# First down product moved behind the next tile's second up product in the early expert steps

## The reference, cut to what matters

```python
x = _layernorm(x, g, b)
x1 = x @ W1 + b1
x2 = jnp.clip(x @ W2 + b2, -20.0, 20.0)
hidden = jnp.clip(x1 * (x2 * jax.nn.sigmoid(x2)), -10000.0, 10000.0)
return jnp.clip(hidden @ Wo + bo, -10000.0, 10000.0)
```

## Time and profile before

| | |
|---|---|
| median of three timed runs | 592.98 us (592.62 to 595.98) |
| profiled execution, its own time | 591.37 us |
| span of the profiled execution | 589.6 us |
| busy share PE / DVE / ACT / POOL | 89% / 84% / 71% / 63% |
| chain that ended last: PE, DVE, issue, ACT | 58%, 16%, 14%, 6% |
| expert stage, step 1 to the last down product | about 322 to 551 us |
| mean granted clock of TensorE | 0.981 |

### The profile page before, as it was taken

How to read it: one execution, slowest core, us unless ns; L and a number is a source line. 1 busy time by engine, 2 the same in 40 slices (tenths; PEclk the granted TensorE clock), 3 DMA queues, 4 the chain that set the end, 5 groups by cost and what they waited for, 6 DMA issues and landing times.

```text
span 589.6 us, 17958 instructions
## 1 busy us (share of the span) xinstructions
PE 527.6 (89%) x5148; PEld 438.5 (74%) x5148; DVE 496.1 (84%) x1548; ACT 419.5 (71%) x1179; POOL 370.9 (63%) x708
## 2 busy tenths in 40 slices
PE   3799999999999999999978888978999999999395
PEld 2577787777877778777657777867898888888295
DVE  2689999999999999999996878889888888877353
ACT  2599998898988989889777654463566666765134
POOL 4325678888888888888877646653544344333344
PEclk9899999999999999999999999998999999999789
DMA  6313213232331311311005445653666666664283
GB/s 178 56 47 81 44 40 92 53 94 50 88 87 58 92 53 48 87 58 56 30 17 173 150 121 161 187 177 107 192 202 187 182 202 203 207 192 153 90 281 94
DMA packets 78933, 68.83 MB, mean 117 GB/s; under 512 B 17092, under 2 KB 60804, under 8 KB 78836
## 3 DMA queue, kind: packets, MB, share of 16 engines
q1 hardware_dynamic: 73748, 57.77, 34.7%
q0 software_dynamic: 4320, 9.15, 4.6%
q10 hardware_dynamic: 768, 0.75, 0.4%
HBM read 52.85 MB, written 14.80 MB: 115 GB/s over the span
## 4 chain that ended last, share of the span: by engine, by line
PE 58%; DVE 16%; issue 14%; ACT 6%; DMA 3%; ACTq 1%; another core or an unknown queue 0%; SPq 0%; DVEq 0%; POOL 0%; POOLq 0%
PE ps_m L845 7%; PE ps_t L785 5%; PE ps_s L785 5%; PE ps_s L825 4%; PE ps_s L827 4%; PE ps_t L827 3%; PE ps_t L825 3%; DVE hid L1461 3%; DVE rinv L1201 3%; PE ps_m L730 2%; ACT sil L1090 2%; PE ps_m L700 2%; PE ps_m L720 2%; PE ps_m L682 2%; PE ps_m L761 2%
## 5 line engine op out<-in xcount | busy, mean ns | idle before, releaser
L845 PEld LDWEIGHTS ps_m<-wot,hid 128*128 128x128 f32 x568 | 83.9, 192 | 20.4 <-issue 7.7
L578 POOL DMA_INDIRECT expert_out<-yt,dest x71 | 70.7, 996 | 43.8 <-issue 23.8
L845 PE MATMUL ps_m<-wot,hid 128*128 128x128 f32 x568 | 91.2, 280 | 7.0 <-DVE yt L1472 3.4
L1025 ACT ACTIVATE sc<-sc,rowmax 128x128 f32<-128x128 f32 x256 | 77.9, 389 | 1.0 <-DVE rowmax L1195 1.0
L1195 DVE TENSOR_REDUCE rowmax<-sc 128x8 f32<-128x1024 f32 x64 | 76.8, 1203 | 0.3 <-issue 0.3
L549 POOL DMA_INDIRECT expert_in<-xhat,pos x64 | 65.0, 1015 | 16.1 <-issue 15.4
L1083 ACT ACTIVATE x2c<-ps_s,prt 128x256 f32<-128x256 f32 (+1 forms) x78 | 35.4, 454 | 54.3 <-PE ps_s L827 48.3
L502 POOL TENSOR_TENSOR sc<-sc,rowmax 128x1024 f32<-128x1024 f32 x32 | 60.7, 1895 | 10.0 <-DVE rowmax L1195 8.7
L1083 ACT ACTIVATE x2c<-ps_t,prt 128x256 f32<-128x256 f32 (+1 forms) x78 | 35.3, 452 | 34.1 <-PE ps_t L827 28.1
L825 PE MATMUL ps_s<-xg,w2t 128*128 128x256 f32 (+1 forms) x156 | 46.5, 380 | 8.5 <-DVE hid L1461 6.7
L568 POOL COPY bot<-bo_rows 128x128 f32 x39 | 11.7, 301 | 60.8 <-DVE yt L1472 60.7
(11 more groups left out here) (283 smaller groups left out, 1576.7 us busy)
## 6 DMA issues: line engine op xcount, KB each, us to landing
w2t<-in_L_ffn_W_dram SPq DMA_DIRECT2D x39, 256.0 KB
w1t<-in_L_ffn_W_dram SPq DMA_DIRECT2D x39, 256.0 KB
wot<-in_L_ffn_Wo_dram SPq DMA_DIRECT2D x39, 256.0 KB
kbd<-key_image SPq DMA_DIRECT2D x29, 256.0 KB
xst<-expert_in SPq DMA_DIRECT2D x32, 137.0 KB
g<-expert_out SPq DMA_DIRECT2D x7, 512.0 KB, 9.1
call<-in_ctx_dram SPq DMA_DIRECT2D x8, 256.0 KB
out_dram<-xall SPq DMA_DIRECT2D x16, 128.0 KB, 1.8
```

The source lines that it names most:

```text
L578: pool.indirect_dma_start(ys_dram[:, :], bass.IndirectOffsetOnAxis(ap=dest[:, n, a:a + 1], axis=0), yt[:, par, a, :], None).then_inc(y_out ...
L845: mm = pe.matmul(ps_y(i)[:, a * P:(a + 1) * P], hid[:, par, c, a * P:(a + 1) * P], wot[:, par, c, :], start=(c == 0 and a == 0), stop=(c = ...
L1025: done = act.activation(sc[:, slot, h, :], sc[:, slot, h, :], ACT.Exp, bias=rowmax[:, slot, h:h + 1])
```

## The change

In steps 1 to 7 TensorE's first down product, of the tile before, is not made behind the first up products but behind the second ones, straight ahead of the second down product. From step 8 on nothing is changed, and no other engine's program differs.

```diff
--- before.py
+++ after.py
@@ -887,7 +887,10 @@
                     for c in range(CH):
                         if has(i, 0):
                             p_up(i, c, par)
-                        if has(i, 1):
+
+                        if has(i, 1) and not (c == 0 and i < MIXED):
+                            if c == 1 and i < MIXED:
+                                p_down(i - 1, 0, 1 - par)
                             p_down(i - 1, c, 1 - par)
                         if c == 1 and has(i, -1):
                             rows(i + 1)
```

## The result

The changed kernel takes 589.66 us (median of 11 runs, 587.45 to 592.52) where the kernel before, run between them on the same chip, takes 592.92 (11 runs, 591.35 to 595.98): ratio 0.9941, 95% interval 0.992 to 0.9963, or 3.5 us less (2.2 to 4.7). Two later comparisons of the same pair gave 0.995 (0.9919 to 0.998) and 0.9945 (0.992 to 0.997). The gain is real and it is half a per cent.

What follows compares the result with a forecast made beforehand. TensorE was taken to bound the kernel, with waits for VectorE's yt in the expert stage. Steps 2 to 7 summed 0.15 + 1.4 + 0.3 + 0.75 + 0 + 0.65 = 3.25 us, taking 592.98 to 589.7 us; range 586.5 to 594.0.

Steps and rivals of the forecast that it cites:

- step 3: Expert stage, step 3: Exp's table load does not wait for gmax, so Exp starts 1.56 us earlier; adds 1.4 us.
- step 4: Expert stage, step 4: gap 0.73 us, but L718 newly waits some 0.35 us for gA; adds 0.3 us.
- step 6: Expert stage, step 6: gap 1.30 us, no slack; ScalarE's 2.79 us pause before its first bias stays; adds 0.
- step 7: Expert stage, step 7: gap 0.67 us under slack 0.77; adds 0.65 us.
- Gap and slack: TensorE, steps 2 to 7: gap is down 0's wait cost, 4.7 us together; slack is up 2's room behind its gate.
- steps 2 and 5: Expert stage: step 2 adds its 0.15 us; step 5, gap 0.83 us under slack 0.86, adds 0.75 us.
- The rival that bet on this: ScalarE's pause in step 6 goes as well, and its gap of 1.30 us is won: 588.4 us, chance 10%.
- I count the wait as gone in every step: TensorE, steps 2 to 7: down 0 behind up 1 no longer waits for yt; 4.7 us of waits together.
- Taken back by the next wait: Rival: VectorE's and ScalarE's waits behind up 2 take the gain back, leaving 1 us: 592.0 us, chance 20%.
- Half clock of step 11 gone: Rival: shifted work misses TensorE's half clock at 400 to 404 us, 1.7 us more won: 586.7 us, chance 5%.
- Slower through pauses: Rival: instruction packets behind weights bring two more 2.7 us pauses at a step's first bias or up product: 595.1 us, 10%.

Runs made afterwards that it cites:

- The step alone: The kernel before with the move made in step 3 alone: 590.63 us against 592.56 for the kernel before, ratio 0.9953.
- twelve instructions more: The changed kernel with twelve 128x1 copies added on ScalarE at the start: 588.93 us against 591.99 for the kernel before, ratio 0.9938.

## Why the prediction was right, and where it was off

The forecast was 589.7 us, 3.3 below before; measured is 589.66, 3.3 below by the medians and 3.5 by the ratio. The clean steps (no pause, full clock) tell how far that is the sum and how far luck. Before, they are 9.20 in step 3, 7.14 in step 4, 7.22 in step 6 and 6.60 in step 7; after, step 4 is 6.99 and step 7 5.87.

| step | 2 | 3 | 4 | 5 | 6 | 7 | sum |
|---|---|---|---|---|---|---|---|
| forecast | 0.15 | 1.4 | 0.3 | 0.75 | 0 | 0.65 | 3.25 |
| measured | 0.17 | 1.43 | 0.15 | 0.77 | 0.72 | 0.73 | 3.97 |

**Gap and slack.** The rule that up 2 can come earlier by the gap as long as the gate lets it gave steps 2 and 5 to 0.02 us. In step 7 it gives 0.63 against the execution that the forecast was read from (forecast 0.65) and 0.73 against the one without a pause, whose wait of 0.49 makes a gap of 0.74. The wait named "issue" in step 7 was the wait for yt: it has that name in the other execution, and it went with the others.

**Step 3** came as worked out, by the table load that doesn't wait for the data of its activation: with the load begun ahead of gmax and Exp right behind it. The step alone gave 1.45, where a load that waits for gmax would have left 0.15 by the prediction's sum. The Trainium skill (ScalarE: Activation LUTs, What ACT_TABLE_LOAD costs) has a drain of 1.38 us for each switch on top of the load; by it this step would have added nothing. The traces speak against that: Exp stands 0.08 us behind its load, and the step gained 1.43.

**Step 4** was mis-sized by a half: 0.15 for 0.3, since the new wait of L718 was put too low. TensorE in the clean step (twelve instructions more):

```profile
347.67 0.59 PE L827 MATMUL ps_s<-xg,w1t 128*128 128x256 f32 x2
348.59 0.46 PE L718 MATMUL ps_m<-vpT,gA 128*128 128x128 f32 x2 [0.32 <-issue]
348.88 0.60 PE L825 MATMUL ps_s<-xg,w2t 128*128 128x256 f32 x2
```

The printed idle of 0.32 looks like the forecast 0.35. But L718 starts 0.49 us later than the 0.43 behind L827, and up 1 follows 0.29 behind it instead of 0.22: 0.56 in all. The prediction added 0.25 to every printed wait of down 0 for these two reasons and left it out for the new one. The gap of 0.73 less 0.56 is 0.17, and the step gained 0.15.

**Step 6 is the term that failed.** "Their place in its stream doesn't change, so I let the pause stay: 0." The step gained 0.72. The pause was not part of the program: of fourteen traces one has it at that length, and where it was it cost 0.23 us, since TensorE was waiting for yt at that time anyway. I had read that the gates hang on the paused bias and concluded that nothing could be won in front of them; another execution of the same kernel would have shown the step without it. The rival that bet on this put the step at its whole gap of 1.30 and got the direction. The rest is in the rows of step 6 above: down 0 still waits for yt there, which costs 0.36 us (0.28 late, 0.08 longer), and the rank product L754 starts 0.37 behind L859 instead of 0.22 and runs 0.07 longer, another 0.22. 1.30 - 0.36 - 0.22 is the 0.72. So "I count the wait as gone in every step" was wrong in this step, where the gap was longer than what up 1 and the small product put in its place.

**Rivals.** Taken back by the next wait: no, 167.10 and 167.19 us from step 8 to the end of the rows. Half clock of step 11 gone: no, in the changed kernel the granted clock is 0.58 in 399 to 403 us, in step 11 as before (0.57). Slower through pauses: the mechanism exists. Of the ten traces of kernels in which step 3's down product stands behind up 1, five show ScalarE standing for 0.79, 1.48, 1.52, 1.56 and 2.30 us ahead of the same bias, straight behind Exp's sum; of the four others none does. Step 3 then takes 8.68 to 10.11 us, so that of its gain of 1.43 at most 0.5 is left; in all five a half clock follows the longer idle time, and step 8 takes 0.25 to 1.1 us more than without. It isn't bound to the chip (one chip has executions with and without), and five of ten against none of four doesn't show that the change brings it. If it did, the change would still gain, as the three comparisons of the pair show. What causes it is open; I tried to move it and it didn't appear.

**Why the median fell on the forecast.** In part by luck. The sum of the clean steps is 3.97, 0.7 above the forecast's, nearly all of it from step 6, and the runs give 3.3 to 3.5. The half clock of step 4 can make up the difference: it costs the changed kernel 1.65 us and the kernel before 1.14, and ten of the fourteen traces have it. Two executions that have it without a pause of ScalarE, one of each kernel (second and fourth line of the table of steps), take 44.12 and 40.65 us for steps 2 to 7, 3.47 apart. Pauses of step 3 would take more. How often the timed runs have either is not known, since they have no traces, so this is argued and not shown.

Two readings of the prediction were off without bearing on the sum. The expert stage is not half of the run but 39% (322 to 551 us). And up 2 of step 6 did stand idle before, 0.2 us that its row doesn't print: it starts 0.35 behind the rank product in front of it, 0.15 in the execution without the pause.

## What to carry to other kernels

When an engine waits for the reader of a shared buffer, put work that doesn't need the buffer ahead of the waiting instruction; the gain of each place is its gap, cut by the slack of the next thing that feeds the engine, and can be read from one trace to 0.05 us. Before a stall in a trace is taken as part of the program, look whether a second execution has it, and what the other engines were waiting for at that moment. A printed idle time is less than what the wait costs; compare the start with where it could have been. For changes of half a per cent compare step lengths rather than spans: two profiled executions differed by 0.5 us where, by the account above, the steps had won 4.

## What the runs showed of the hardware that was not expected

ScalarE's table load runs ahead of its activation's wait: it began 1.04 us before the reduction that the activation waits for. With two loads in a step this makes an earlier bias worth its full 1.4 us.

ScalarE can stand for 0.8 to 2.8 us with its semaphore reached and its data there, at one place in some executions and not in others of the same or nearly the same program. The Trainium skill (Runtime: NRT & Kernel Launch, Instruction fetch mechanics) says that fetching instructions ahead mostly hides its cost. Whether these pauses are such fetches no run here shows: in the five executions with the pause of step 3 an instruction packet began 2.5 to 3.2 us before ScalarE went on; in the five of the changed order without it the same packet began 0.6 to 1.2 us before that bias, which excludes that the bias always has to wait so long for it.

A stretch of some 3.4 us at the 1.2 GHz level came behind 1.6 to 4.0 us of idle TensorE at the head of step 4 in some executions of both kernels and not in others (1.6 us idle in two of the changed kernel's, with 8.65 and with 6.99 us for the step; 2.1 in two of the kernel before, with 8.28 and with 7.14). It cost 1.65 us in the one and 1.14 in the other, where part of it fell into a wait.
